# Two row biases moved from GpSimd additions into products of one row on TensorE, in the last stream of a language-model tower

## What is computed

```
def retention_core(xn, decay_logit, W_out, b_out, conv_w, conv_b):
    a = sigmoid(decay_logit)
    s = a * s + (1.0 - a) * xt              # scan over the tokens
    y_ret = einsum('btd,ed->bte', ss, W_out) + b_out
    y_loc = conv(xc, conv_w)                # 5 taps along the tokens, each feature alone
    return y_ret + (y_loc + conv_b)

y = retention_core(layernorm(x, ln1_g, ln1_b), ...)
x = x + y
h = layernorm(x, ln2_g, ln2_b)
h = gelu(einsum('btd,hd->bth', h, W1) + b1)
y = einsum('bth,dh->btd', h, W2) + b2
return x + y
```

## Time before, and how to read the profile

| | |
|---|---|
| median of 3 runs | 993.16 us (992.84 to 994.09) |
| profiled execution | 995.26 us, span 993.5 us |
| mean granted TensorE clock | 0.93 |
| final stream, turns 0 to 26 | about 803 to 910 us of the span |
| busy over the span | PE 84%, ACT 60%, DVE 60%, POOL 55% |

### The profile page before, as it was taken

One profiled execution on the slowest core, in us unless ns is written; L12 is line 12 of the kernel. 1 busy time (PEld: TensorE's weight loads), 2 busy tenths in 40 slices (PEclk: granted clock), 3 DMA queues, 4 the chain that ended last, 5 costly groups with the idle time before them and its releaser, 6 DMA issues.

```text
span 993.5 us, 23915 instructions
## 1 busy us (share of the span) xinstructions
PE 833.4 (84%) x8499; PEld 634.8 (64%) x8499; DVE 592.4 (60%) x1891; ACT 597.0 (60%) x1654; POOL 550.0 (55%) x823
## 2 busy tenths in 40 slices
PE   2899988979899889499998897989989958873775
PEld 0677756657777557277775666777756737762775
DVE  2588845338987352369873523888634357976342
ACT  1579984338899733277998333889963235642443
POOL 2458875533588652255886533358855355576242
PEclk9899997989999999799999798999988969995898
DMA  2210004102000060131000500200006050001220
GB/s 80 76 45 3 4 16 136 52 8 79 3 4 3 20 182 1 40 91 29 4 3 20 172 10 12 76 3 4 4 20 181 1 192 1 1 34 54 70 77 22
DMA packets 39251, 45.46 MB, mean 46 GB/s; under 512 B 7313, under 2 KB 34032, under 8 KB 38978
## 3 DMA queue, kind: packets, MB, share of 16 engines
q1 hardware_dynamic: 17706, 20.59, 7.1%
q10 hardware_dynamic: 19156, 18.60, 6.5%
q0 software_dynamic: 2272, 4.74, 1.5%
HBM read 22.10 MB, written 21.59 MB: 44 GB/s over the span
## 4 chain that ended last, share of the span: by engine, by line
PE 61%; DVE 14%; ACT 7%; issue 6%; DMA 6%; POOL 4%; POOLq 1%; ACTq 1%; SPq 1%; DVEq 0%
PE bank L1448 6%; PE bank L1385 5%; PE bank L1458 4%; PE bank L1459 4%; PE bank L1409 4%; PE bank L1336 4%; PE bank L1278 4%; PE bank L1388 3%; ACT p L720 3%; PE bank L1339 3%; PE bank L1289 3%; DMA xt<-xs 3%; DMA wqb<-in_wqkv 2%; PE bank L1257 2%; PE bank L1258 2%
## 5 line engine op out<-in xcount | busy, mean ns | idle before, releaser
L575 POOL TENSOR_TENSOR p<-p 128x384 f16<-128x384 f32 (+1 forms) x320 | 270.3, 857 | 107.3 <-ACT p L720 98.6
L958 DVE TENSOR_REDUCE nmx<-bank 128x1 f32<-128x384 f32 (+1 forms) x384 | 190.8, 512 | 32.6 <-PE bank L1339 28.2
L719 ACT ACTIVATE p<-bank 128x384 f32<-128x384 f32 (+1 forms) x384 | 174.0, 453 | 40.4 <-PE bank L1388 26.1
L720 ACT ACTIVATE p<-bank 128x384 f16<-128x384 f32 (+1 forms) x384 | 174.5, 455 | 0.0
L1385 PE MATMUL bank<-stack 103*128 103x128 bf16 x1056 | 144.6, 221 | 1.8 <-ACT stack L731 0.7
L1388 PE MATMUL bank<-bandb,idb 128*128 128x128 bf16 x672 | 135.0, 221 | 0.0
L1336 PE MATMUL bank<-stack 100*128 100x384 bf16 (+1 forms) x384 | 119.8, 312 | 1.6 <-DVE nmx L958 1.3
L1409 PE MATMUL bank<-vst,p 128*128 128x49 bf16 x2112 | 114.7, 185 | 0.0
L1385 PEld LDWEIGHTS bank<-stack 103*128 103x128 bf16 x1056 | 88.0, 98 | 26.2 <-issue 16.3
L1339 PE MATMUL bank<-bandb,idb 128*128 128x128 bf16 x672 | 100.5, 218 | 0.0
L1409 PEld LDWEIGHTS bank<-vst,p 128*128 128x128 f16 x2112 | 90.9, 97 | 9.1 <-issue 0.8
(11 more groups left out here) (259 smaller groups left out, 1887.4 us busy)
## 6 DMA issues: line engine op xcount, KB each, us to landing
xs<-zrow ACTq DMA_DIRECT2D x8, 2193.0 KB, 14.3
xt<-xs SPq DMA_DIRECT2D x23, 129.0 KB, 2.1
w2s<-in_w SPq DMA_DIRECT2D x4, 576.0 KB
mwbs<-in_mwb SPq DMA_DIRECT2D x1, 2064.0 KB, 8.6
mw2s<-in_mw SPq DMA_DIRECT2D x1, 2048.0 KB, 12.9
lnrow<-in_lnr SPq DMA_DIRECT2D x4, 480.0 KB
stack<-mtr SPq DMA_DIRECT2D x96, 3.0 KB
wqb<-in_wqkv SPq DMA_DIRECT2D x6, 218.2 KB
```

The costliest lines, as they stand in the source:

```text
L575: nc.gpsimd.tensor_tensor(p2[:, u % RING, 0:w], p32[:, u % RING, 0:w], p1[:, u % RING, 0:w], ALU.subtract).then_inc(p2_pool, 1)
L719: nc.scalar.activation(p32[:, s % RING, 0:w], ps[2 + s % 3][:, 0:w], ACT.Exp).then_inc(p32_ready, 1)
L720: nc.scalar.activation(p1[:, s % RING, 0:w], ps[2 + s % 3][:, 0:w], ACT.Exp).then_inc(p1_ready, 1)
L958: nc.vector.tensor_reduce(nmx[:, vn % 3, h:h + 1], nat_bank(v)[:, 0:w], AX.X, ALU.max, negate=True).then_inc(max_done, 1)
```

## The change

GpSimd's additions L618 and L619 go, and with them the semaphore `xb_ready` and DVE's and POOL's waits on it. In their place one product of a row of ones with the bias row opens each of two accumulations: `ab2b` in bank 3 ahead of L1496, and `bo2b` in bank 4 ahead of L1505. The products that came first keep their place and now add to what is in the bank.

```diff
             for t in range(NN + DEPTH + BPQ + 1):
-                i = t - 4
-                if 0 <= i < NN:
-                    pool.wait_ge(z1_ready, i + 1)
-                    nc.gpsimd.tensor_tensor(h0[:, i, :], h0[:, i, :], ab2b[:, :], ALU.add)
-                    nc.gpsimd.tensor_tensor(x1[:, i, :], x1[:, i, :], bo2b[:, 0, :], ALU.add).then_inc(xb_ready, 1)
                 i = t - 7
                 if 0 <= i < NN:
-                    pool.wait_ge(xb_ready, i + 1)
                     pool.wait_ge(y_added, i + 1)
                     nc.gpsimd.tensor_tensor(h0[:, i, :], h0[:, i, :], x1[:, i, :], ALU.add).then_inc(xh_ready, 1)
@@
                     dve.wait_ge(c_mm, i + 1)
-                    dve.wait_ge(xb_ready, i + 1)
                     nc.vector.tensor_tensor(x1[:, i, :], ps[4][:, 0:DM], x1[:, i, :], ALU.add).then_inc(y_added, 1)
@@
                     pe.wait_ge(gelu_done, i + 1)
                     if i:
                         pe.wait_ge(x_added, i)
+                    mm(ps[3][:, 0:DM], ones[0:1, 0:P], ab2b[0:1, :], start=True, stop=False)
                     for m in range(2):
-                        ins = mm(ps[3][:, 0:DM], gl[:, i % 2, m, :], aw2s[:, m, :], start=m == 0, stop=m == 1)
+                        ins = mm(ps[3][:, 0:DM], gl[:, i % 2, m, :], aw2s[:, m, :], start=False, stop=m == 1)
                     ins.then_inc(m2_mm, 1)
@@
                     if i:
                         pe.wait_ge(y_added, i)
+                    mm(ps[4][:, 0:DM], ones[0:1, 0:P], bo2b[0:1, 0, :], start=True, stop=False)
                     for k in range(KC):
-                        mm(ps[4][:, 0:DM], xn[:, b, n * P + k:(n + 1) * P + k], diag[:, k, :], start=k == 0, stop=False)
+                        mm(ps[4][:, 0:DM], xn[:, b, n * P + k:(n + 1) * P + k], diag[:, k, :], start=False, stop=False)
                     pe.wait_ge(scan_done, i + 1)
                     mm(ps[4][:, 0:DM], st[:, i % 4, :], wos[:, :], start=False, stop=True).then_inc(c_mm, 1)
```

More of the change, by code:

```diff
@@ L346, in program @@
         c_mm = sem("c_mm")
-        xb_ready = sem("xb_ready")
         y_added = sem("y_added")
```

## The result

| | before | after |
|---|---|---|
| median (range), same chip | 993.0 us (991.3 to 994.1, 4 runs) | 1015.98 us (1010.9 to 1018.9, 4 runs) |
| ratio, 95% interval | | 1.0228 [1.0184, 1.0271] |
| profiled execution | 995.26 us, span 993.5, clock 0.930 | 1010.92 us, span 1009.2, clock 0.921 |
| full turn, from one L1532 (after: L1526) to the next | 4.64 us | 5.16 us |

The forecast was 1001.7, with a range up to 1005.0. The direction is right, and the time lies 14.3 us beyond the forecast and 11.0 us beyond the top of the range.

The account below looks back on a forecast made before the run. DVE and POOL bound full turns (4.64 us), PE and ACT late ones (4.14); 0.97 a turn of bias products makes PE and ACT decide at 5.11. Shifts +3.8 through turn 16 and +4.7 late give +8.5: 993.16 to 1001.7, range 994.8 to 1005.0.

Parts of the forecast that it names:

- The ring: Last stream: chain of waits setting a turn; DVE and POOL at 4.64 us before, PE and ACT at 5.11 after.
- its hand-over: Full turns: PE and ACT take over from DVE and POOL, losing 0.47 us a turn.
- the loss at few rows: PE, around each bias product: about 0.10 us lost going in and 0.10 coming out, plus 0.10 for empty starts.
- DVE and POOL ring: Full turns: without POOL's additions DVE normalises faster, about 0.29 us a turn, 4.64 to 4.35.
- Rivals 2: Empty start unpaid in changes to and from few rows: 0.72 us a turn, turn 4.86, 998.2 us; chance 0.12.
- 3 (4.6 for one row): No loss from few rows: 0.44 us a turn, PE and ACT at 4.58, 993.9 to 995.9 us; chance 0.10.
- 4 (4.36): One-row passes mostly hidden: both products 0.22 us a turn, DVE decides at 4.36, about 990 us; chance 0.04.
- turns 14, 15 and 16: DVE's choosing and placing fits under PE's turns, then full clock in turn 16: shift +4.7 to +4.0 to +3.8.
- turns 21 and 22: End of the late turns: only bank 3's bias is paid, 2 x 0.40 us.
- I expect the clock to hold: Turn 16: PE later and fuller, one gap of about 0.7 us instead of two; turn 5.97 us against 6.13.
- rival 1: Half clock in turn 16 after all: 1.6 us not saved, bias products at half clock; +2.4, 1004.1 us; chance 0.25.
- The last turns, the tables and the experts run as before: After turn 22: nothing changes there, only moved later by the summed shift of +8.5 us.

Follow-up runs that it names:

- full_rows: Changed kernel with each bias product given 128 rows (identity times bias tile) instead of one; 994.62 us, ratio 0.9997 to before.
- switch_only: As full_rows, plus behind each bias product a one-row product of 8 columns of zeros; 1013.76 us, ratio 1.0187 to before.
- no_switch: As full_rows, plus behind each bias product a 128-row product of 8 columns of zeros; 1002.33 us, ratio 1.0062 to before.
- one_row_again: The changed kernel unaltered, measured and profiled on another occasion; 1008.44 us, ratio 1.0142 to before.
- rows_64: As full_rows with only 64 rows, so the bias reaches only the first 64 tokens of each block; 1006.25 us, ratio 1.0109 to before.
- rows_32: As full_rows with only 32 rows, so the bias reaches only the first 32 tokens of each block; 1009.62 us, ratio 1.0151 to before.
- rows_33: As full_rows with only 33 rows, so the bias reaches only the first 33 tokens of each block; 1008.29 us, ratio 1.0116 to before.
- bank3_only: Changed kernel keeping only bank 3's one-row bias product, bank 4's bias given back to POOL as an addition; 1000.59 us, ratio 1.0052 to before.
- bank4_only: Changed kernel keeping only bank 4's one-row bias product, bank 3's bias given back to POOL as an addition; 1005.07 us, ratio 1.0109 to before.
- rows_65: As full_rows with only 65 rows, so the bias reaches only the first 65 tokens of each block; 993.25 us, ratio 0.9975 to before.
- ahead_full: Changed kernel with both bias products given 128 rows and moved to the end of PE's turn, where PE waits; 989.16 us, ratio 0.9935 to before.
- ahead_one: Changed kernel with both one-row bias products moved to the end of PE's turn, where PE waits; 990.23 us, ratio 0.9942 to before.
- no_bias: Changed kernel with both bias products dropped and no POOL additions, so neither bias is added; 990.31 us, ratio 0.9961 to before.

## Why the prediction was right in its direction and short in its size

**The ring, its hand-over and the loss at few rows: right.** Forecast and measured: bank 3 0.40 and 0.41, bank 4 0.57 and 0.61, full turn 5.11 and 5.16, DVE and POOL ring 4.35 and 4.34, normalisations 0.26 and 0.27 apart, POOL's wait above 3 and 3.56. Rivals 2 (turn 4.86), 3 (4.6 for one row) and 4 (4.36) fall by the turn of 5.16. The loss going in and coming out that I read off products of 24 rows is shown to be that of the rows, by full_rows and again by switch_only against no_switch.

**The schedule at the least half clock.** The profile of one_row_again is 11.0 us above that of before at the same half clock over the whole (137 against 139), though with 6 us more of it in the stream. By L1526 and L1532, measured with the forecast's terms behind:

| stretch | change | forecast |
|---|---|---|
| up to the second L1526 (1.2 to the first) | +2.2 | +1.7 |
| the next five (25.80 for 22.58) | +3.2 | +3.0 |
| turns 14, 15 and 16 (17.82 for 17.05) | +0.8 | -0.9 |
| three late turns (15.40 for 12.42) | +3.0 | +2.9 |
| turn 20 | +1.0 | +1.0 |
| turns 21 and 22 (3.21 + 4.64 for 5.60) | +2.3 | +0.8 |
| the rest of the stream | +0.3 | 0 |
| sum | +12.8 | +8.5 |

The sum is 1.8 above the 11.0 of the whole profile: the rest of the program ran that much shorter than in before, with 8 us less of half clock. The terms that the ring gives are met to about 0.5. Two fail, and most of both is clock. "I expect the clock to hold" in turn 16: it fell in all three profiles of this kernel. The turn took 7.50 in two of them and 8.37 in the third. With the clock held it took 5.91 in no_switch, which has 5.03 - 4.14 = 0.89 a turn to pay, and 6.49 in switch_only, which has 1.46; between them the changed kernel with its 1.02 would come to about 6.0, an estimate, and the forecast for it was 5.97. So about 1.5 is the lower clock, and the hand-over to GELU was estimated to about 0.1. That is rival 1, at part of its price. In the last two turns one product ran at the lower level, 4.64, and in rows_64 at the full one, 3.21.

**The step that failed most: the clock elsewhere.** I let the clock change in turn 16 alone, and "The last turns, the tables and the experts run as before". The first measurement's median execution has 174 us of half clock, the profile of the table 137; 37 x 0.30 is 11 us (9 to 13 by the interval). Of the 14.3 that were missing these are the larger part. The table's stream exceeds the forecast by 4.3, and the 1.8 that the rest of that profile ran shorter go off again: 13.5 in all. The price of each us comes from executions of the same kernel, where nothing else was altered; that such terms, taken on different chips, may be added is argued, not shown.

**What stays open.** Why one-row products go with more half clock. It is not the length of the turn alone: rows_64 has the same 5.16 and stayed at 138 (137 to 143). It is not the change of rows alone: switch_only has as many changes and 140. Both have few executions beside a kernel that itself ran between 136 and 181, so neither is excluded by a wide margin. Falls in the middle of the running stream were in the profiles of the one-row kernel, rows_32, rows_33, rows_64, bank3_only and bank4_only, and in none of full_rows, rows_65, ahead_full, ahead_one and no_bias, one profile each. But few rows aren't needed for one: before has a fall at 870.7, and no_switch, all of whose bias products have 128 rows, one from 896.8 to 903.7, where its turn took 8.35; switch_only has one at 906.5. What made the first measurement (median 174) differ from the two later ones (151 and 156) is open as well.

## What to carry to other kernels

Before a product with few rows is put into a running stream of TensorE, ask for its place and its rows: at 64 rows or fewer it costs 0.29 us more each time here, which identity times a replicated tile avoids at the same number of matmul instructions. A bias that opens an accumulation depends on nothing but its free bank, so it can be issued where PE already waits; there it was free, and the relief of GpSimd and VectorE was worth 0.65%. Relieving the engine that waits last is worth only what the next ring allows: 0.5 us a turn of slack on PE and ACT was all there was, against 1.02 added.

## What was not expected of the hardware

The loss at few rows is a step between 64 and 65 (turn 5.16 and 4.59), not a slope, and two passes of 8 columns in float32 cost as much as two of 128, 0.22 us. The granted clock fell in the middle of a running stream (at 838.7, behind 5.32 busy us of 6.60), and one kernel with the same turns at the full level took from 1005.3 to 1020.1 us, with 136 to 181 us of it at the lower level.
